# A graph network kernel: the edge-mean products of two MLP units issued as a pair, each in its own half of TensorE's rows

## The reference, cut to what matters

```
h = maximum(layernorm(x), 0)                                   # [6250, 256]
agg = segment_sum(edge_features, dst) / maximum(counts, 1)     # [6250, 64]
x = x + relu(concat([agg, h], axis=1) @ W1 + b1) @ W2 + b2     # W1 [320, 512], W2 [512, 256]
h = maximum(layernorm(x), 0)
x = x + h @ w_self.T + b_self + (segment_sum(h[src], dst) / maximum(deg, 1)) @ w_neigh.T
```

## Time and profile before

| | |
|---|---|
| median of three runs | 1198.36 us (1198.36 to 1198.54) |
| the profiled execution, its own time | 1198.31 us |
| its span | 1196.4 us |
| edges with MLP steps 0 to 6 | to about 347 us of the span |
| MLP steps 7 to 11 | 361.9 to 457 us |
| the last unit's first product | 457 to 462 us |
| neighbour sums and layer 1 | 462 us to the end |

### The profile page before, as it was taken

One profiled execution on the slowest core, in us unless ns is written; L12 is line 12 of the kernel. 1 busy time (PEld: TensorE's weight loads), 2 busy tenths in 40 slices (PEclk: granted clock), 3 DMA queues, 4 the chain that ended last, 5 costly groups with the idle time before them and its releaser, 6 DMA issues.

```text
span 1196.4 us, 31423 instructions
## 1 busy us (share of the span) xinstructions
PE 1125.3 (94%) x11714; PEld 856.3 (72%) x11714; DVE 815.7 (68%) x1813; ACT 520.3 (43%) x987; POOL 419.8 (35%) x384
## 2 busy tenths in 40 slices
PE   3689999999979997999999999999999999999996
PEld 2677787778768886677677677767777777776774
DVE  6877787787762578677576766766757666676661
ACT  4435555333212465444344444444444444444441
POOL 3111111110006640545345354443634535353461
PEclk9899999999988998899999999999999999999998
DMA  7766655555551210212122121221212212121121
GB/s 245 236 195 202 187 158 158 158 158 160 165 192 49 77 58 18 71 58 76 47 65 67 58 70 53 61 61 53 78 48 66 62 53 71 51 70 58 54 78 32
DMA packets 66875, 116.15 MB, mean 97 GB/s; under 512 B 10463, under 2 KB 30643, under 8 KB 66781
## 3 DMA queue, kind: packets, MB, share of 16 engines
q1 hardware_dynamic: 51740, 75.12, 20.3%
q0 software_dynamic: 15040, 39.80, 11.9%
HBM read 101.93 MB, written 12.95 MB: 96 GB/s over the span
## 4 chain that ended last, share of the span: by engine, by line
PE 81%; DVE 7%; issue 4%; DVEq 3%; ACT 3%; DMA 2%; ACTq 0%; SPq 0%
PE bank L1176 35%; PE couples L1169 10%; PE couples L1008 8%; PE bank L1195 7%; PE bank L966 5%; PE bank L955 5%; PE bank L953 3%; PE couples L1013 2%; PE bank L1187 2%; PE bank L1207 1%; DMA kreg<-in_edge_attr_dram 1%; PE couples L922 1%; DVE oreg L1617 1%; ACT hbuf L677 1%; DVEq L1484 1%
## 5 line engine op out<-in xcount | busy, mean ns | idle before, releaser
L1176 PE MATMUL bank<-hreg,areg 128*128 128x512 f16 x2058 | 504.7, 382 | 0.0
L597 POOL DMA_INDIRECT wide<-h_table,aggn x280 | 324.8, 1160 | 408.8 <-PE couples L1169 194.1
L807 ACT ACTIVATE areg<-couples 128x784 bf16<-128x784 f32 x336 | 276.7, 824 | 369.7 <-PE couples L1169 367.5
L1176 PEld LDWEIGHTS bank<-hreg,areg 128*128 128x128 bf16 x2058 | 265.7, 144 | 104.5 <-issue 1.1
L1617 DVE TENSOR_TENSOR hids<-iota,kreg 128x1024 bf16<-128x1024 f16 x336 | 196.6, 626 | 48.8 <-PE couples L1169 48.7
L1617 DVE TENSOR_TENSOR oreg<-iota,kreg 128x1024 bf16<-128x1024 f16 x336 | 195.9, 624 | 46.2 <-PE couples L1169 44.8
L1008 PEld LDWEIGHTS couples<-oreg,kreg 128*64 128x64 f32 x3232 | 116.9, 142 | 63.8 <-issue 62.8
L1008 PE MATMUL couples<-oreg,kreg 128*64 128x48 f32 x3232 | 138.3, 230 | 20.3 <-DVE oreg L1369 14.7
L1369 DVE TENSOR_TENSOR oreg<-iota,wide 128x384 f32<-128x384 f32 x202 | 122.3, 606 | 4.4 <-issue 1.3
L564 POOL TENSOR_TENSOR xr<-xr,b2bc 128x512 f32 x25 | 33.2, 1326 | 224.9 <-ACT h0buf L687 224.9
L1169 PEld LDWEIGHTS couples<-oreg 128*128 128x128 bf16 x1344 | 76.8, 98 | 49.3 <-issue 13.6
(11 more groups left out here) (167 smaller groups left out, 1069.0 us busy)
## 6 DMA issues: line engine op xcount, KB each, us to landing
kreg<-in_edge_attr_dram SPq DMA_DIRECT2D x202, 256.0 KB, 2.7
h_table<-hreg SPq DMA_DIRECT2D x25, 256.0 KB
xr<-in_x_dram SPq DMA_DIRECT2D x6, 1024.0 KB, 7.5
out_dram<-hbuf SPq DMA_DIRECT2D x42, 128.0 KB
wide<-h_table,aggn POOLq DMA_INDIRECT x280
wide<-in_L_gnn_W_dram SPq DMA_DIRECT2D x2, 512.0 KB, 8.5
out_dram<-h0buf SPq DMA_DIRECT2D x6, 128.0 KB
hreg<-in_dst_dram SPq DMA_DIRECT2D x1, 512.0 KB
```

The lines of the kernel that those rows point to most:

```text
L597: pool.indirect_dma_start(near[:, k, :], None, table, bass.IndirectOffsetOnAxis(ap=nearsrc[:, n * GHALF + k:n * GHALF + k + 1], axis=0)).t ...
L807: act.activation(step.rearrange("p (a k) -> p a k", a=2), cpl[s % 2][:, :, 0:BC * KEYS], ACT.Copy).then_inc(s_adj, 1)
L1176: ins = pe.matmul(bank[4 + par], adj[:, par, :, h], htab[:, h, :], start=(h == 0), stop=(h == TN - 1))
```

## The change

The zero halves go. `w1a` holds the 64 rows of `W1` twice, in rows 0 to 63 and 64 to 127 (two DMAs in place of one), and the mean of q=0 is written to the upper half of `aggn`, that of q=1 to the lower half. The products of line 953 become 64 rows deep: for each block the one of q=0 (rows 0 to 63) and the one of q=1 (rows 64 to 127) are issued one behind the other, then come the two products with `w1b` of q=0, then those of q=1.

The order of the pieces becomes block by block: at j = 0 the two mean products and the `w1b` products of q=0, at j = 1 the `w1b` products of q=1, and so on at 3 and 4, 6 and 7, 9 and 10. A step therefore ends its use of `aggn` for both units at j=9.

Both units have banks of their own in each stage (`hidden_bank`): 4 and 5 beside the edges, where block pair k=1 waits for the ReLU of k=0; 4, 5, 2 and 3 behind them. The product with `W2` waits for the first half of `hids` and then, in its second half, for the rest. ScalarE's `hidden` goes by k, then q.

Behind the edges `inverses(i + 1)` comes after the `hidden` products of its step. The last unit uses `own=2`: four single mean products of 64 rows, each before the two `w1b` products of its block. GpSimd's memsets of `w1a` and of `aggn` are gone, and SyncE waits for one memset in place of two. The waits on `s_w` count nine DMAs in place of eight (these lines are left out here, as are unchanged ones).

```diff
@@ -370,6 +370,10 @@
+        def hidden_bank(q, k, own):
+            return bank[(4 + q, 4 + q - 2 * k, 4 + k)[own]]
         def later(i):
@@ -433,7 +437,9 @@
                 sp.dma_start(bsbc[:, :], bself.rearrange("(a n) -> a n", a=1).broadcast_to([P, D])).then_inc(s_w, 16)
-                sp.dma_start(w1a[0:FE, :], w1[0:FE, :]).then_inc(s_w, 16)
+                for q in range(2):
+                    sp.dma_start(w1a[q * FE:(q + 1) * FE, :], w1[0:FE, :]).then_inc(s_w, 16)
                 sp.dma_start(w1b[:, :, :], w1[FE:FE + D, :].rearrange("(h p) n -> p h n", p=P)).then_inc(s_w, 16)
@@ -441,7 +447,7 @@
-            sp.wait_ge(s_zero, 2)
+            sp.wait_ge(s_zero, 1)
             load_x(0)
@@ -518,7 +524,6 @@
             pool.memset(xr[:, TF:T, :], 0.0).then_inc(s_zero, 1)
-            pool.memset(w1a[:, :], 0.0).then_inc(s_zero, 1)
             pool.memset(viol[:, :], 0.0)
@@ -552,8 +557,6 @@
             pool.memset(acc[:, :], 0.0).then_inc(s_const, 1)
-            pool.memset(aggn[:, :, :], 0.0)
             pool.wait_ge(s_idx_act, CH)
@@ -651,14 +654,14 @@
-            def hidden(i, q, own=0):
-                if later(i):
-                    act.wait_ge(s_outp[q], i)
-                for k in range(2):
+            def hidden(i, k, own=0):
+                for q in range(1 if own == 2 else 2):
+                    if k == 0 and later(i):
+                        act.wait_ge(s_outp[q], i)
                     act.wait_ge(s_hidp[q], 2 * i + k + 1)
                     for b in range(2):
-                        ins = act.activation(hids[:, q, 2 * k + b, :], bank[4 + k - 2 * q * own][:, b * NM:(b + 1) * NM],
+                        ins = act.activation(hids[:, q, 2 * k + b, :], hidden_bank(q, k, own)[:, b * NM:(b + 1) * NM],
                                              ACT.Relu, bias=b1T[:, 2 * k + b:2 * k + b + 1])
@@ -776,7 +779,7 @@
             def layer0(i, n=None):
-                hidden(i, 0)
+                hidden(i, 0, own=1)
                 hidden(i, 1, own=1)
@@ -791,13 +794,14 @@
                 layer0(KEY0 + n, n)
-            hidden(U // 2 - 1, 0)
+            hidden(U // 2 - 1, 0, own=1)
             hidden(U // 2 - 1, 1, own=1)
             copy_places(2)
-            hidden(U // 2, 0)
+            hidden(U // 2, 0, own=2)
+            hidden(U // 2, 1, own=2)
@@ -933,45 +937,49 @@
-            def hidden(i, q, k, b, own=0):
+            def hidden(i, k, b, q, own=0):
+                cols = slice((2 * k + b) * P, (2 * k + b + 1) * P)
+                if q == 0:
+                    qs = range(1 if own == 2 else 2)
+                    for e in qs:
+                        if b == 0:
+                            if k == 0:
+                                if not later(i):
+                                    pe.wait_ge(s_const, 2)
+                                pe.wait_ge(s_agg[e], i + 1)
+                            if own or k == 1 or later(i):
+                                pe.wait_ge(s_hids[e], 2 * i + (k - (own > 0)))
+                    for e in qs:
+                        pe.matmul(hidden_bank(e, k, own)[:, b * NM:(b + 1) * NM], w1a[e * FE:(e + 1) * FE, cols],
+                                  aggn[e * FE:(e + 1) * FE, e, :], start=True, stop=False)
+                    if k == 0 and b == 0:
+                        pe.wait_ge(s_h0T, 2 * i + len(qs))
                 u = 2 * i + q
-                if k == 0 and b == 0:
-                    if not later(i) and q == 0:
-                        pe.wait_ge(s_const, 2)
-                    pe.wait_ge(s_agg[q], i + 1)
-                    pe.wait_ge(s_h0T, 2 * i + q + 1)
-                if b == 0:
-                    if own:
-                        pe.wait_ge(s_hids[q], 2 * i + (k - 1))
-                    elif q == 1:
-                        pe.wait_ge(s_hids[0], 2 * i + (k + 1))
-                    elif later(i):
-                        pe.wait_ge(s_hids[1], 2 * i + (k - 1))
-                o = bank[4 + k - 2 * q * own][:, b * NM:(b + 1) * NM]
-                cols = slice((2 * k + b) * P, (2 * k + b + 1) * P)
-                pe.matmul(o, w1a[:, cols], aggn[:, q, :], start=True, stop=False)
                 for h in range(DH):
-                    ins = pe.matmul(o, w1b[:, h, cols], h0T[:, bass.ds(2 * u, 2), h, :], start=False, stop=(h == DH - 1))
+                    ins = pe.matmul(hidden_bank(q, k, own)[:, b * NM:(b + 1) * NM], w1b[:, h, cols],
+                                    h0T[:, bass.ds(2 * u, 2), h, :], start=False, stop=(h == DH - 1))
                 if b == 1:
-                if t == 0 and half == 0:
-                    if later(i):
+                if t == 0:
+                    if half == 0 and later(i):
                         pe.wait_ge(s_x1[q], i)
-                    pe.wait_ge(s_hids[q], 2 * i + 2)
+                    pe.wait_ge(s_hids[q], 2 * i + 1 + half)
                 for b in range(half * HB // 2, (half + 1) * HB // 2):
-            def all_hidden(i, q):
+            def all_hidden(i, own=1):
                 for k in range(2):
                     for b in range(2):
-                        hidden(i, q, k, b, own=1)
+                        for q in range(1 if own == 2 else 2):
+                            hidden(i, k, b, q, own)
@@ -979,7 +987,7 @@
-            pieces = [(hidden, q, k, b) for q in range(2) for k in range(2) for b in range(2)]
+            pieces = [(hidden, k, b, q) for k in range(2) for b in range(2) for q in range(2)]
             pieces += [(outer, q, t, half) for q in range(2) for t in range(2) for half in range(2)]
@@ -1124,9 +1132,8 @@
             def layer0(i, n=None):
+                all_hidden(i)
                 inverses(i + 1)
-                for q in range(2):
-                    all_hidden(i, q)
                 all_outer(i, 0)
@@ -1134,7 +1141,8 @@
-            pe.wait_ge(s_hids[1], 2 * BESIDE)
+            for q in range(2):
+                pe.wait_ge(s_hids[q], 2 * BESIDE)
             pe.wait_ge(s_h0T, U)
@@ -1208,7 +1216,7 @@
-            all_hidden(U // 2, 0)
+            all_hidden(U // 2, own=2)
             for s in range(ST):
@@ -1381,7 +1389,7 @@
                     dve.wait_ge(s_hidp[q], 2 * i)
-                dve.tensor_tensor(aggn[0:FE, q, :], acc[0:FE, bass.ds((2 * i + q) * NM, NM)], deg[:, :],
+                dve.tensor_tensor(aggn[q * FE:(q + 1) * FE, q, :], acc[0:FE, bass.ds((2 * i + q) * NM, NM)], deg[:, :],
                                   ALU.mult).then_inc(s_agg[q], 1)
@@ -1451,7 +1459,7 @@
                 dve.wait_ge(s_hidp[q], 2 * i)
-                dve.tensor_tensor(aggn[0:FE, q, :], acc[0:FE, (2 * i + q) * NM:(2 * i + q + 1) * NM],
+                dve.tensor_tensor(aggn[q * FE:(q + 1) * FE, q, :], acc[0:FE, (2 * i + q) * NM:(2 * i + q + 1) * NM],
                                   bank[0][0:FE, q * NM:(q + 1) * NM], ALU.mult).then_inc(s_agg[q], 1)
             def layer0(i, n=None, means=all_means):
```

More of the change, by code:

```diff
@@ L566, in _ @@
             with pool.If(in_windows(pool)):
-                pool.wait_ge(s_w, 8 * 16)
+                pool.wait_ge(s_w, 9 * 16)
                 loop(pool, add_b2, 0, U)
@@ L1049, in _ @@
                 loop(pe, groups, 1, H0[0])
-                pe.wait_ge(s_w, 8 * 16)
+                pe.wait_ge(s_w, 9 * 16)
                 span(0)
```

## The result

The changed kernel takes **1192.04 us** (median of 5 runs, 1188.83 to 1193.50) where the kernel before, beside it, takes 1198.36 (5 runs, 1196.68 to 1198.54): ratio 0.9941, 95% interval [0.9927, 0.9955]. It is 0.6% faster, 6.3 us. The forecast was 1199.8, 1.5 us slower and too little to tell from no change; the time lies at the rival "whole overlap" (1191.9). The profiled execution took 1192.04 as well, with a span of 1190.1 us (before: 1196.4).

What follows compares the result with a forecast made beforehand. TensorE bounds the stage beside the edges and steps 7 and 8; steps 9 to 11 wait for VectorE's keys. Terms -0.5 + 1.5 + 0.3 + 1.6 - 0.4 - 1.0 = +1.5 on 1198.31: 1199.8 us, this case spanning 1197.5 to 1203.

Steps and rivals of the forecast that it cites:

- whole overlap: Faster rival: the two 64-row products of a pair take 0.43 us together; 1191.9 us in all, chance 0.15.
- the pair: Two 64-row mean products on TensorE: half overlap by queue order, three records, 0.65 us, saving 0.217 us.
- the start: VectorE's conversion, held up by GpSimd's memsets, ends earlier without two of them, and all that follows too: -1.0 us.
- Changes of shape: TensorE going between 64 and 128 rows: 0.20 us for each new change.
- the cheap changes: Faster rival: half overlap and 0.10 us a change of shape, 1194.3 us; with 0.07, 1193; chance 0.17.
- the dear ones: Slower rival: changes of shape cost 0.29 us each, 1206.4 us in all; chance 0.08.
- Beside the edges: Seven steps with 28 block pairs, each saving 0.217 us and paying 0.20 for one new change: -0.5 us.
- Behind the edges: Steps 7 and 8, 8 pairs with two new changes each: +1.5 us; steps 9 to 11, less slack: +0.3.
- The last unit: No partner for its products, so four times 0.40 us with nothing back, on the ReLU's path: +1.6 us.
- Inverse counts: Moved behind the `hidden` products, so those of step 7 start without waiting for VectorE's start indices: -0.4 us.
- New waits: VectorE's mean at j=10 waiting for TensorE, ScalarE emptying banks and the outer product's earlier wait: all 0.

Runs made afterwards that it cites:

- e6: As e5, but with all upper-half products ahead of all lower-half products in each stretch of 64-row products: 1194.29 us, ratio 0.9953 to the kernel before.
- e5: Changed kernel with mean products last for b=0 and first for b=1, so 64-row products stand together, beside and behind the edges and in the last unit: 1193.28 us, 0.9948.
- g1: Changed kernel with pairs beside the edges alone; steps 7 to 11 and last unit at 128 rows in the old order: 1189.63 us, once more 1191.90.
- e3: Changed kernel with both GpSimd memsets and the wait for both put back: 1194.11 us, ratio 0.9952 to the kernel before.
- e4: Changed kernel with the inverse counts ahead of a step's first products again: 1192.81 us, ratio 0.9944 to the kernel before.
- f1: Changed kernel with 64-row products of b=0 and b=1 together beside the edges, VectorE's second inverse and mean of q=0 at j=10 and 11: 1193.46 us, 0.9942.
- f3: As f1, also 64-row products together in the last unit, and second inverse and mean of q=1 at j=17 and 18: 1190.67 us, 0.9908.
- g3: Changed kernel with VectorE's second inverse and mean of q=1 two slots later, at j=17 and 18: 1187.54 us, ratio 0.9902 to the kernel before.

## Why the prediction was wrong, point by point

**The step that failed: the pair.** "If starts keep their order, the order of records is A1, A2, B1, B2: A2 and B1 can overlap, A1 and B2 stand alone. [...] I take 0.217, by the order of the queue." Starts do not keep their order between opposite halves: A1 and B1 begin together, then A2 and B2, and the pair saves 0.43. e6 shows it more sharply, since the lower half there starts past records of the upper that had not started. The evidence used for the order, the quarters of columns in the earlier trace rows, had one record for each quarter in turn and could not tell "in order" from "in any order". The missing 0.217 for each of 36 pairs is 7.8 us, which is the distance from 1199.8 to 1192.04. The rival "whole overlap" had the price right (28 x -0.23) and got a chance of 0.15, with that same order counted against it. That its total (1191.9) came so near is in part luck: beside the edges 6.4 were forecast and 5.9 came, the start was forecast at -1.0 and the stage began 0.4 later, and what follows the last unit became 0.7 shorter without a term for it.

**Changes of shape: right.** 0.20 was taken by the earlier trace rows; the new one beside the edges costs 0.20, and e5 gives 0.20 (1.19 for six changes) and about 0.2 (one). That rules out the cheap changes (0.10 or 0.07) and the dear ones (0.29).

**Beside the edges: right but for the pair.** 0.23 a pair, 0.93 a step, 6.5 us in seven by the steady step; 5.9 were there from the first product to the last group, since the first two steps gave less (0.58 and 0.69: 39.78 and 39.89 us, before 40.36 and 40.58).

**Behind the edges: right but for the pair.** A pair of blocks costs 2.55 (by the forecast's terms 2.60 - 0.217 + 0.40 = 2.78). The waits for keys are 0.92, 0.57 and 0.75 us, no shorter than the 0.85, 0.56 and 0.61 of the earlier trace rows: steps 9 to 11 are VectorE's as before. The last unit was forecast at +1.6 and costs 6.66 - 5.24 = 1.42; g1, with full depth there, is back at 5.24.

**Inverse counts (-0.4) and start (-1.0): not settled.** The products of step 7 do follow the start sums without the old 0.62 us of waiting. The conversion has two parts, and the forecast's 12.12 is the end of the first; that one now ends at 11.19, near the 11.1 forecast, and the second at 11.78 (before 12.71). The first part ends 0.55 us behind the end of GpSimd's last memset in both kernels (12.12 behind 11.57, now 11.19 behind 10.64), which bears out that GpSimd held it up. By their ratios e3 and e4 lie 1.3 and 0.4 us above the changed kernel, with intervals that overlap its own. That "all that follows hangs on the conversion" is seen up to the first groups only: by the first pair, executions of one kernel differ by more than that (2.4 us), for a reason that these runs do not show.

**New waits at 0: right in the stage, incomplete behind it.** VectorE's mean at j=10 does wait for TensorE, 1.19 us in the step looked at, and no group waits for a comparison at j=11, as worked out. What the forecast did not look at was the ReLU of k=1 of q=0 behind the edges, whose time until `outer` shrank from over 5 us to 1.1. It costs nothing in the profiles where increments arrive in time.

## What to carry to other kernels

Two products of half the depth in opposite halves of TensorE's rows cost as much as one, also when each is two records. Issue them alternately, and don't reckon with the queue's order between them. In all runs here the two wrote to different PSUM banks; one bank was not tried. Each change between half and full depth costs 0.2 us with float32 weights of 128 columns, so the pair (0.43) pays for one such change and breaks even at two. Where a unit has no partner, leave it at full depth. When an engine on the path is relieved, read what every other engine is late with by then: here a comparison held up by GpSimd ate what joined visits save beside the edges, and moving one inverse and one mean of VectorE by two slots gave more than any of those runs.

## What the runs showed of the hardware that was not expected

Opposite halves of the rows start out of the queue's order, past four records of the other half but not past eight (in e6, 0.97 us alone, then together). A VectorE comparison that begins while GpSimd's addition runs ends 0.40 to 0.43 us after it, whenever it began. That is so for all 53 stretched comparisons between 120 and 330 us in six of the kernels (before, changed, e5, f1, f3, g3), with 0.91 to 1.62 us in place of 0.56; those that began in the addition's last 0.1 us took their usual 0.56. In some executions TensorE's increments seem to reach ScalarE and VectorE 1 to 4 us late behind the edges, on one chip in all four kernels; what delays them no run here shows. And in four executions of one kernel the first product beside the edges lies anywhere from 70.3 to 72.7 us; the mean granted clock from 20 to 72 us (0.87 or 0.90) does not sort them.
